# A binary search for 64 medians inside a fused convolution and attention kernel: one product and one clamp per step

## What is computed

```python
def _L0_conv_ref(x, lpf):
    B, C, H, W = x.shape
    q_in = jnp.quantile(x.reshape(B, C, -1), 0.5, axis=-1)
    x = x + jax.nn.relu(-q_in)[:, :, None, None]
    y = upfirdn2d(x, lpf, up=2, padding=6, gain=4.0)
    y = jnp.maximum(y, 0.0)
    return upfirdn2d(y, lpf, down=2, padding=0, gain=1.0)
```

## Time and profile before

| what | value |
|---|---|
| median of 3 runs | 11891.15 us (11887.46 to 11897.37) |
| the profiled execution | 11873.21 us, span 11871.9 us |
| TensorE busy | 89% of the span |
| VectorE busy | 74% |
| ScalarE busy | 61% |
| GpSimd busy | 22% |
| TensorE's granted clock, mean | 0.977 of full |
| steps of the search | 26 in the prologue, 26 in each of 16 passes: 442 |

### The profile page before, as it was taken

How to read it: one execution, slowest core, us unless ns; L and a number is a source line. 1 busy time by engine, 2 the same in 40 slices (tenths; PEclk the granted TensorE clock), 3 DMA queues, 4 the chain that set the end, 5 groups by cost and what they waited for, 6 DMA issues and landing times. The chain is left out here.

```text
span 11871.9 us, 199727 instructions
## 1 busy us (share of the span) xinstructions
PE 10619.5 (89%) x72913; PEld 5396.2 (45%) x72913; DVE 8837.9 (74%) x15501; ACT 7247.2 (61%) x12109; POOL 2639.5 (22%) x4368
## 2 busy tenths in 40 slices
PE   1898998989989899898989989899898998989989
PEld 1544535344453544535435354453534445454453
DVE  6777777777777777777777777777777777777776
ACT  4656566665656656566565665656566565665656
POOL 1222313122131221312213121221312213122130
PEclk9999999999999999999999999999999999999999
DMA  2021120312212022130211202122021221202213
GB/s 56 27 43 48 42 66 20 53 38 48 60 30 57 23 53 56 33 62 24 50 51 40 65 23 45 46 44 64 24 53 34 50 59 30 57 23 54 55 34 74
DMA packets 176585, 537.89 MB, mean 45 GB/s; under 512 B 64873, under 2 KB 87401, under 8 KB 154033
## 3 DMA queue, kind: packets, MB, share of 16 engines
q1 hardware_dynamic: 175664, 525.24, 19.6%
HBM read 232.43 MB, written 71.30 MB: 26 GB/s over the span
## 5 line engine op out<-in xcount | busy, mean ns | idle before, releaser
L963 DVE TENSOR_REDUCE R<-ps 128x2 f32<-128x640 f32 x4096 | 3184.4, 818 | 880.3 <-PE ps L699 879.7
L1170 ACT ACTIVATE R<-ps 128x512 f32<-128x512 f32 x5120 | 2820.2, 594 | 638.7 <-PE ps L720 613.1
L247 ACT ACTIVATE R<-R,st 128x1475 bf16<-128x1475 f32 (+1 forms) x1326 | 2077.5, 1567 | 663.8 <-DVE st L316 639.0
L304 DVE TENSOR_SCALAR_CACHE_REDUCE R<-R,st 128x1255 bf16<-128x1255 f32 (+1 forms) x1326 | 1937.3, 1461 | 19.6
L699 PE MATMUL ps<-KST,R 96*128 96x320 bf16 x8192 | 1799.1, 300 | 35.7 <-DVE R L963 32.8
L745 PE MATMUL ps<-R 128*32 128x512 f32 x12288 | 1634.0, 604 | 37.9 <-DVE Wk L916 32.8
L720 PE MATMUL ps<-R,KST 104*128 104x512 bf16 x4096 | 1562.3, 384 | 37.6 <-ACT R L1170 28.0
L699 PEld LDWEIGHTS ps<-KST,R 96*128 96x128 bf16 x8192 | 753.9, 98 | 728.6 <-DVE R L963 218.6
L1253 POOL CAST R<-Wk 128x512 bf16<-128x512 f32 x256 | 283.8, 1109 | 2464.6 <-DVE Wk L916 2464.6
L720 PEld LDWEIGHTS ps<-R,KST 104*128 104x128 bf16 x4096 | 393.7, 97 | 718.6 <-ACT R L1170 467.6
L473 PE MATMUL ps<-R,cst 64*128 64x512 f32 x2048 | 570.3, 630 | 113.1 <-ACT R L1064 111.3
(11 more groups left out here) (208 smaller groups left out, 19297.2 us busy)
## 6 DMA issues: line engine op xcount, KB each, us to landing
R<-R SPq DMA_DIRECT2D x3072, 64.0 KB, 2.4
R<-xh_in SPq DMA_DIRECT2D x136, 512.0 KB, 4.4
out_dram<-Z SPq DMA_DIRECT2D x68, 1024.0 KB, 3.9
R<-xa_in SPq DMA_DIRECT2D x36, 1024.0 KB, 11.3
R<-xb_in SPq DMA_DIRECT2D x36, 1024.0 KB, 11.7
R<-sr_in SPq DMA_DIRECT2D x32, 1024.0 KB, 5.2
R<-sr_in SPq DMA_DIRECT2D x16, 2016.0 KB, 10.3
R<-sr_in SPq DMA_DIRECT2D x16, 1056.0 KB
```

Of the source, the lines that this page charges most:

```text
L247: e.activation(junka[:, 0:o2 - o1], xc[:, o1:o2], ACT.Sign, bias=mid, scale=-1.0, accum_out=cnt[:, NP + i:NP + i + 1]).then_inc(md_ca, 1)
L304: e.tensor_scalar(junk[:, 0:o1 - o0], xc[:, o0:o1], mid, None, ALU.is_le, ALU.add, accum_out=cnt[:, i:i + 1]).then_inc(md_cv, 1)
L963: e.tensor_reduce(MX[(4 * u + s4) % 2][:, blk_, h0:h0 + 2], ps[:, 2 + 2 * bq:4 + 2 * bq, 0:320], axis=AX.X, op=ALU.max).then_inc(mx, 1)
L1170: e.activation(PB[:, t % 2, w, :], ps[:, w % 2, :], ACT.Exp).then_inc(ex, 1)
```

## The change

A new constant `pairbig` is `pair` times -2^100. ScalarE's three counts, VectorE's three and constants lie in one row of columns, and one product reads two overlapping windows of this row (5 columns each in steps 0 to 20, 6 each in the last five), so that VectorE's columns are read twice. A constant column holds the limit, offset by 0.25. The sum of the 10 or 12 product columns is then a huge positive or a huge negative number. The new `mid` is min(max(sum, mid - hs/2), mid + hs/2) in one VectorE operation with two per-partition operands. GpSimd makes these two ends, `ends`, in two one-element operations per step, right behind the step's `lift`; they wait for `md_v`, and the clamp waits for them (`md_ends`). `lift` compares with 0. The semaphore `md_got` no longer stands between two VectorE operations of a step. The constants grow by 128 columns; `row` moves into `Wk`; the prologue gets three small memsets.

```diff
-                e.matmul(P0(2 * NP), lhsT=c("pair"), rhs=cnt[:, 0:2 * NP], start=True, stop=False)
-                e.matmul(P0(NP), lhsT=c("pair"), rhs=cnt[:, 0:NP], start=False, stop=True).then_inc(md_p, 1)
+                e.matmul(P0(2 * WINDOWS[k][2]), lhsT=c("pairbig"), rhs=counts(k), start=True, stop=True).then_inc(md_p, 1)
...
+WINDOWS = [(1, 2, 5) if k < 21 else (0, 3, 6) for k in range(STEPS)]
+        def counts(k):
+            a, stride, n = WINDOWS[k]
+            first = st[:, 80 + a:81 + a]
+            return bass.AP(first.tensor, first.offset, [list(first.ap[0]), [stride, 2], [1, n]])
...
+                if k < STEPS - 1:
+                    e.wait_ge(md_v, 2 + k)
+                    e.tensor_tensor(ends[:, 0:1], mid, hs[:, k + 2:k + 3], ALU.subtract)
+                    e.tensor_tensor(ends[:, 1:2], mid, hs[:, k + 2:k + 3], ALU.add).then_inc(md_ends, 1)
                 for _ in range(NP):
                     yield
                 e.wait_ge(md_g, 2 + k)
...
-                e.tensor_scalar(lift, gg, FEWER[k], BIG, ALU.is_lt, ALU.mult).then_inc(md_lift, 1)
+                e.tensor_scalar(lift, gg, 0.0, BIG, ALU.is_gt, ALU.mult).then_inc(md_lift, 1)
...
-                e.tensor_reduce(gg, P0(2 * NP), axis=AX.X, op=ALU.add).then_inc(md_g, 1)
+                e.tensor_reduce(gg, P0(2 * WINDOWS[k][2]), axis=AX.X, op=ALU.add).then_inc(md_g, 1)
                 if k < STEPS - 1:
                     e.wait_ge(md_g, 2 + k)
-                    e.tensor_scalar(uu, gg, FEWER[k], hs[:, k + 1:k + 2], ALU.is_lt, ALU.mult).then_inc(md_got, 1)
-                    e.wait_ge(md_got, 2 + k)
-                    e.scalar_tensor_tensor(then, uu, hs[:, k + 2:k + 3], mid, ALU.subtract, ALU.add).then_inc(md_v, 1)
+                    e.wait_ge(md_ends, k + 1)
+                    e.tensor_scalar(then, gg, ends[:, 0:1], ends[:, 1:2], ALU.max, ALU.min).then_inc(md_v, 1)
```

More of the change, by code:

```diff
@@ L72, in program @@
         W = sb("Wk", [128, 3072])
-        st = sb("st", [128, 88])
+        st = sb("st", [128, 92])
         sB = sb("sB", [128, C])
         ones = sb("ones", [64, 128])
-        row = sb("row", [1, 128])
         selk = sb("selk", [64, 3, 4, 96], BF16)
@@ L92, in program @@
         dg = W[0:64, 2560:2624]
+        row = W[0:1, 2880:3008]
         XH = [(R4, R2)[k // 4][:, o:o + 1024].rearrange("p (c w) -> p c w", c=8)
@@ L164, in program @@
         segs = ((0, 256, "1", VP1, 16), (256, 320, "2", VP2, 8))
-        lo, cnt, gg, hi = st[:, 0:1], st[:, 80:88], st[:, 9:10], st[:, 11:12]
+        lo, gg, hi = st[:, 0:1], st[:, 9:10], st[:, 11:12]
         pm, other, hs = st[:, 12:14], st[:, 14:16], st[:, 16:16 + STEPS + 1]
-        mm, mids, lift, uu = st[:, 64:80], st[:, 46:48], st[:, 48:49], st[:, 10:11]
+        mm, mids, lift, ends = st[:, 64:80], st[:, 46:48], st[:, 48:49], st[:, 6:8]
         m1 = st[:, 50:54]
+        less2, less1 = st[:, 80:81], st[:, 87:88]
+        cv = [st[:, 83 + i:84 + i] for i in range(NP)]
+        ca = [st[:, o:o + 1] for o in (81, 82, 86)]
+        def counts(k):
+            a, stride, n = WINDOWS[k]
+            first = st[:, 80 + a:81 + a]
+            return bass.AP(first.tensor, first.offset, [list(first.ap[0]), [stride, 2], [1, n]])
         def P0(n, rows=128):
@@ L220, in pe_median @@
             b7.free(e)
-            e.matmul(P0(1), lhsT=c("pair"), rhs=cnt[:, 0:1], start=True, stop=True).then_inc(md_p, 1)
+            e.matmul(P0(1), lhsT=c("pair"), rhs=cv[0], start=True, stop=True).then_inc(md_p, 1)
             b7.ask()
@@ L345, in dve_median @@
             e.tensor_scalar(gg[0:64], gg[0:64], -0.5, 0.5, ALU.mult, ALU.add).then_inc(md_got, 1)
-            e.wait_ge(md_got, STEPS + 1)
+            e.wait_ge(md_got, 2)
             e.tensor_tensor(v2, v2, gg[0:64], ALU.mult).then_inc(md_got, 1)
-            e.wait_ge(md_got, STEPS + 2)
+            e.wait_ge(md_got, 3)
             e.tensor_tensor(q, v2, hi[0:64], ALU.add).then_inc(md_got, 1)
-            e.wait_ge(md_got, STEPS + 3)
+            e.wait_ge(md_got, 4)
             e.tensor_scalar(q, q, -1.0, 0.0, ALU.mult, ALU.max).then_inc(md_got, 1)
-            e.wait_ge(md_got, STEPS + 4)
+            e.wait_ge(md_got, 5)
             e.tensor_scalar(dg, c("ident", 64)[:, 0:64], q, None, ALU.mult).then_inc(md_row, 1)
@@ L1352, in first_tensor @@
             e.wait_ge(in_c, 16)
-            e.wait_ge(vm, 1)
+            e.wait_ge(vm, 2)
             for _ in pe_median(e, Bank7()):
@@ L1365, in first_vector @@
             e.memset(ones[:, :], 1.0).then_inc(vm, 1)
+            e.memset(less2, 0.5 * (FEWER[0] - FEWER[21]))
+            e.memset(less1, 0.25 - 0.5 * FEWER[0])
+            e.memset(st[:, 88:89], 0.0).then_inc(vm, 1)
             e.memset(Z[:, :, :], 0.0)
@@ L1451, in host_layout @@
     put("edft", np.concatenate([(np.cos(half) * wt)[:, 0:64].T, -(np.sin(half) * wt)[:, 1:65].T], 0) * r)
+    put("pairbig", (n[:, None] % 64 == n[None, :] % 64) * -BIG)
     put("halves", np.tile(2.0 ** (1 - np.arange(STEPS + 1)), (128, 1)))
```

12 lines of the change are left out of this document (6 added, 6 removed).

## The result

The changed kernel takes 11678.9 us (median; 11661.3 to 11689.4) where the kernel before takes 11891.4 beside it: ratio 0.9818, interval 0.9806 to 0.9829. The forecast was 11689 us, in a range of 11625 to 11775. The total came out 10 us under the forecast, which is closer than its terms deserve. The steps of the search gave 10.2 us a pass where 10.35 had been forecast, but the part behind them lost 2.7 us, where this part and the clock together had been put down for a gain of 1.2, and the start of a pass, which I had not priced at all, gave 3.3 us.

What follows compares the result with a forecast made beforehand. TensorE, busy for 89% of the span, was taken to bound the kernel. Savings of 169 us in 16 passes, 17.4 in the prologue and 16 from the clock made 202 us, so 11689 us, in a range of 11625 to 11775.

Steps and rivals of the forecast that it cites:

- The product: Search step: one accumulating product fewer saves 0.44 us of latency in the prologue, 0.22 in the filter stage, 0.18 in forward transform.
- step 16: Search step in the forward transform, whose middle holds ScalarE while TensorE idles: forecast to save 0.25 + 0.14 = 0.39 us.
- The second operation: End of a search step: the clamp replaces line 314 and saves line 316's 0.25 us, at no extra cost.
- chain step: Steps 1, 4, 5, 6, 8 to 11, 19, where TensorE waits on line 316: 0.47 us each, 4.23 a pass.
- The stall: Line 316 held by GpSimd in steps 2, 13 and 14 to 16, 18; the clamp, a scalar form, counted as free.
- first rival: The clamp is held by GpSimd like line 316: 24 us stay, 11713 us; chance 0.12.
- Step 2: Search step where line 316 takes 1.20 us: forecast 0.22 of product plus 1.24 from line 316, 1.46 us.
- The clock: Shorter waits make stretches at 1.2 GHz rarer: 1 us a pass, 16 us in all.
- The prologue: Bare chain of search steps: 26 x 0.44 + 25 x 0.25 = 17.7 us, less 0.3 for larger constants, 17.4.
- Product only: Rival: only the product counts, the earlier middle's gain is lost in the next wait; 109 us, 11782 us; chance 0.07.
- The slower one: Rival: the clamp waits 0.9 us for GpSimd's late ends in each of 425 clamps; 12071 us; chance 0.02.

## Why the prediction was right

*The product.* Forecast 0.44 us of latency in the prologue, 0.22 with the clock up. Measured 0.41 and 0.22. In the forward transform I took 0.18 of TensorE and the same of latency; there is no gain in latency at all (0.54 us from product to sum in both kernels), since VectorE's own copy ends last. TensorE's time there falls by 0.22 a step. In step 16, priced at 0.39 us with the latency, only these 0.22 came: TensorE's idle time before the product of step 17 stayed at 2.0 us in each of 16 passes. The timeline of step 15 of the changed kernel:

```profile
1144.98 0.28 PE L213 MATMUL ps<-st,cst 128*128 128x10 f32 x2
...
1145.17 0.43 DVE L885 COPY R<-ps 128x260 f32<-128x260 f32 x1 [0.19 <-PE ps L551]
1145.52 0.16 DVE L324 TENSOR_REDUCE st<-ps 128x1 f32<-128x10 f32 x1
```

*The second operation.* Forecast 0.25 us, with 0 to 0.05 over line 314 for the clamp, and I took 0. Measured 0.19: the clamp costs 0.06 over line 314, at the upper bound and slightly past it. It shows in every chain step: the nine chain steps came to 3.91 in place of 4.23 us (0.41 in six of them, which is 0.22 + 0.19; 0.90, 0.36 and 0.19 in steps 4, 11 and 19, and the 0.90 is 0.41 where no stretch at 1.2 GHz falls into it), and a step of the prologue to 0.61 in place of 0.69. The reason I gave for zero, that line 304 waits for two semaphores too, was about waits; the price is that of a second per-partition operand, for which the trace of before had no row.

*The stall.* The clamp is never held, so the first rival is out, and the rule of the Trainium skill on the shared port (SBUF — State Buffer, "Who interferes with whom") shows here for two tensors only; the scalar form, which by that page can enter a mode that takes the pair too if its operands allow it, was never held. Step 2 gave 2.11 us, not 1.46: the wait that it took away had a slow-clock stretch behind it in 9 of 15 passes. Without such a stretch it gave 1.17 us, and all of that by the clamp: the run of the clamp alone shows the same 10.18 us for this step, so the 0.22 us of product that I added there did not come.

*The pass start.* I gave it nothing, and it gave 3.32 us, nearly a third of the gain of a pass. It belongs to no step of the search. The kernel before gets as much from moved code, 54 us, where the change brings 212. Compared with the moved kernel before, whose branch is short too, the change is worth 11828 - 11679 = 149 us, or 161 by the two ratios.

*The clock.* I forecast 1 us a pass of gain, with bounds of 3.8 both ways. The sum of slow clock fell a little (33.2 to 30.9 us a pass), but the stretches moved. At the start of a pass there are 3.9 us less of them, in step 2 2.1 us less and in step 4 1.1 us less; behind step 25, where TensorE is the bound, 5.5 us more. In the steps that brought some 0.9 us a pass (steps 2 and 4 gained 1.4 over what they give without a stretch, steps 14 and 17 lost 0.4), at the start of a pass some 1.5, which I count with the branch, and the part behind step 25 lost 2.7, some 1.9 of it by the clock. So apart from the start it was a loss of about 1 us, not a gain of 1. That the waits get shorter was right; that stretches then become rarer where they cost did not follow. The range, too, was cut short on this side: it took 40 us for the lower bound of the clock where the prediction had named 61.

*The prologue.* Forecast 17.4 us, measured 14.1: 25 steps of 0.61 us are 15.2, and the first image comes 1.0 us later (28.3 to 29.3 us), not 0.3. In the other runs with the larger constants the first product starts 0.3 to 1.1 us later than before.

*The rivals.* Product only: refuted by the run of the clamp alone. The slower one: refuted by the doubled ends. So the sum for the search and the clock, 202 us, was too high by a quarter to a third against 149 to 161, and the code's place brought it back. By the table the steps themselves came out nearly as priced; what is missing lies behind step 25. That 3.3 us won at the start stand against 2.7 lost behind step 25 is luck: with the branch moved the changed kernel takes 11697 us, with all places as before 11754. The two runs that did one part each gained 0.83 and 0.56%, 1.39 together where the change gains 1.82: both carry more time at 1.2 GHz a pass (36.2 and 37.5 us) than the whole change does (30.9).

## What to carry to other kernels

Before a gain is put down to an edit, read the time at the start of the loop, where nothing was edited: a loop of thousands of instructions can win or lose 2 us a turn at its closing branch, and more with the clock behind it, by where its code lies, and a kernel with idle instructions ahead of the loop is the control that shows it. Read the passes one by one before taking a mean or a median: a part of a pass has two or three lengths, by whether a stretch at 1.2 GHz falls into it. Price a saved wait together with the clock: behind the stall of 1.0 us in step 2 a stretch at 1.2 GHz cost 1.6 us more in 9 of 15 passes. Filling the idle stretches ahead of such ones with dead products of 512 float32 columns (0.89 us each) and a few smaller ones brought 70 us, a third of what the change brought. An operation of one column pays for its form: two tensors can be held up by GpSimd for 1 us, two per-partition scalars cost 0.06 us always.

## What the runs showed of the hardware

- TensorE's loop branch takes 0.36 to 0.49, 1.07 to 1.29 or 1.85 to 3.05 us for the same jump, and the kernel before gains 54 us from 152 more instructions ahead of its loop.
- A branch that takes over 1 us ends 2.5 to 3.0 us after the start of a 16 KB packet of code that was fetched around it, in 84 of 84 cases.
- A one-column TENSOR_SCALAR of float32 takes 0.214 us with one per-partition operand and 0.273 with two, in 425 of 425 cases each, inside GpSimd's additions of 512 columns as well.
- A one-column SCALAR_TENSOR_TENSOR takes 0.220 us, and up to 1.20 while GpSimd adds tensors of 512 columns.
- An instruction that waits for semaphores long past their value takes 0.05 us on TensorE, and the next one starts 0.11 us after its start.
- The part of a pass behind step 25 loses some 0.36 us for each us at 1.2 GHz (420.2 us with none, 426.3 with 17).
